# Sixteen-graph network with neighbour dilation: keep-masks written in place with two stores per graph, adjacency rows loaded from ScalarE's queue

## Time and profile before

| | |
|---|---|
| median of 3 runs | 2692.42 us |
| lowest, highest | 2684.85, 2693.45 us |
| the profiled execution, its own time | 2686.08 us |
| its span, first to last instruction | 2684.3 us |
| what lies around the span | 1.8 us |
| mean granted clock of PE | 0.990 of full speed |

### The profile page before, as it was taken

How to read it: one execution, slowest core, us unless ns; L and a number is a source line. 1 busy time by engine, 2 the same in 40 slices (tenths; PEclk the granted TensorE clock), 3 DMA queues, 4 the chain that set the end, 5 groups by cost and what they waited for, 6 DMA issues and landing times. The chain is left out here.

```text
span 2684.3 us, 38830 instructions
## 1 busy us (share of the span) xinstructions
PE 2574.4 (96%) x12390; PEld 1634.7 (61%) x12390; DVE 2082.9 (78%) x5413; ACT 1365.9 (51%) x4060; POOL 598.8 (22%) x265
## 2 busy tenths in 40 slices
PE   6999989999989999999999998999999999999898
PEld 4666656656655666656665664555555555555797
DVE  5788889889889988989989877766666635666676
ACT  4566645665654676646663421332322344443676
POOL 0000000000000000000000003766666603433673
PEclk8999999999999999999999999999999999999999
DMA  7254184364177347157345223555555419996663
GB/s 246 79 164 132 48 201 136 97 158 155 43 197 194 89 146 192 49 157 198 93 113 159 46 69 137 201 192 192 192 191 191 183 55 387 405 404 261 251 234 152
DMA packets 325878, 455.48 MB, mean 170 GB/s; under 512 B 155680, under 2 KB 218528, under 8 KB 325664
## 3 DMA queue, kind: packets, MB, share of 16 engines
q1 hardware_dynamic: 325664, 452.89, 52.4%
HBM read 352.13 MB, written 67.11 MB: 156 GB/s over the span
## 5 line engine op out<-in xcount | busy, mean ns | idle before, releaser
L721 PE MATMUL a_acc<-a_ew,a_Hr 128*128 128x512 f32 x1536 | 754.4, 600 | 0.0
L895 DVE TENSOR_TENSOR a_ew<-adj,a_cos 128x512 f32<-128x512 f32 x768 | 508.0, 681 | 69.0 <-PE a_cos L714 67.1
L712 PE MATMUL a_cos<-a_nh 128*128 128x512 f32 x768 | 417.2, 543 | 31.5 <-DVE a_ew L895 16.4
L721 PEld LDWEIGHTS a_acc<-a_ew,a_Hr 128*128 128x128 f32 x1536 | 275.8, 190 | 153.7 <-issue 110.2
L641 POOL TENSOR_TENSOR a_Au<-a_Ab,tri 128x512 fp8e4<-128x512 fp8e4 x32 | 36.8, 1150 | 1367.2 <-ACT a_Ab L815 1367.2
L832 ACT ACTIVATE a_v<-a_D,a_wb,a_small 128x256 f16<-128x256 f32 x512 | 287.2, 632 | 99.8 <-PE a_D L754 59.9
L714 PE MATMUL a_cos<-a_nh,a_nl 128*128 128x512 f32 x768 | 305.5, 398 | 0.0
L713 PE MATMUL a_cos<-a_nl,a_nh 128*128 128x512 f32 x768 | 302.9, 394 | 0.0
L822 ACT ACTIVATE a_vr<-a_D,a_small 128x128 f16<-128x128 f32 x432 | 161.9, 457 | 134.1 <-DVE a_small L967 133.8
L1387 PE MATMUL b_acc<-adj,b_z 128*128 128x512 f32 x512 | 225.0, 592 | 0.0
L712 PEld LDWEIGHTS a_cos<-a_nh 128*128 128x128 f32 x768 | 146.1, 190 | 127.5 <-DVE a_ew L895 52.7
(11 more groups left out here) (267 smaller groups left out, 4361.3 us busy)
## 6 DMA issues: line engine op xcount, KB each, us to landing
adj<-in_adjT SPq DMA_DIRECT2D x108, 1024.0 KB, 12.6
adj<-in_adjT SPq DMA_DIRECT2D x128, 512.0 KB, 4.0
stage<-in_adj SPq DMA_DIRECT2D x256, 256.0 KB, 3.3
scr_keep<-a_kp SPq DMA_DIRECT2D x256, 64.0 KB, 1.8
scr_z<-b_zT SPq DMA_DIRECT2D x32, 512.0 KB, 3.7
scr_ag<-b_a SPq DMA_DIRECT2D x32, 512.0 KB, 3.3
stage<-scr_keep SPq DMA_DIRECT2D x13, 1024.0 KB, 7.3
b_kp<-scr_keep SPq DMA_DIRECT2D x12, 1024.0 KB, 7.8
```

The costliest lines, as they stand in the source:

```text
L712: e.matmul(cos[j][:], n[:, blk(k)], n[:, half(j)], start=True, stop=False)
L721: e.matmul(acc[j][:], Hr[u % 2][:, k, :], ew[idx % EW][:], start=(k == 0), stop=(k == NK - 1)).then_inc(E["agg"], 1)
L895: e.tensor_tensor(ew[idx % EW][:], adj[g % 2][:, k, half(j)], cos[j][:], ALU.mult).then_inc(E["ew"], 1)
```

## The change

- The mask is written in place: the product goes back to the half row of `TT` that it reads. The three buffers `kp` and the 256 stores go. Once all eight rows of one half of a graph are masked, SP stores that half (512 KB, 4096 bytes of each partition in one piece), two stores per graph, each graph of a quad with a semaphore of its own (`st0` to `st3`). The scratch tensor gets the layout of `TT`, so the second stage reads the masks with a step of two bytes (`masked`), and a graph's masks are 8 KB in one piece on each partition.
- New order constraints: a mask waits for the flips that still read what it overwrites (`flips_ahead`), on the diagonal also for the block's `check`; a flip waits for masks released ahead of it (`masks_ahead`). A `fill` of quads 2 and 3 waits for both stores of its graph in the quad before. A graph's flips and masks at a block are placed graph by graph, all flips ahead of the masks.
- The adjacency rows are loaded by ACT instead of SP: a step `load` in ACT's order, from which the step `row` takes it. The plan has it at 90 ns on ACT and 1000 ns of transfer (before: 70 on SP and 700).
- `PACE` goes from 24 to 22, and there is one more semaphore.

The core of the diff (the fallback `dilate_all`, which this trace doesn't run, gets the same layout):

```diff
-PACE = 24
+PACE = 22
+MASK = 3
-        S["keep"] = nc.dram_tensor("scr_keep", [G, NK, 128, N], U8, kind="Internal").ap()
+        S["keep"] = nc.dram_tensor("scr_keep", [G, 128, NK * N], U8, kind="Internal").ap()
-def readers(quad, i, k):
-    seen = [(q, k // 4) for q in range(NK)] + [(k, 1 - k // 4)]
-    return [("dve", "mask", quad, i, q, j) for q, j in seen]
+def released(m, j):
+    return max(2 * m + 1, 4 * j + 3)
+def crossing(q, j):
+    return [(m, q // 4) for m in (2 * j, 2 * j + 1)]
+def flips_ahead(q, j):
+    return [f for f in crossing(q, j) if released(*f) <= released(q // 2, j)]
+def masks_ahead(m, j):
+    return [(q, h) for q in range(NK) for h in range(2)
+            if (m, j) in crossing(q, h) and released(q // 2, h) < released(m, j)]
...
-            freed = readers(quad - 2, i, k) if quad > 1 else []
+            freed = [("dma", "store", quad - 2, i, j) for j in range(2)] if quad > 1 else []
             for j in range(2):
-                transfer(("row", n, i, j), 700, early + ([("dve", "wide", prev, i, j)] if done else []),
-                         None, "af")
-                add("act", ("row", n, i, j), 540, 2, [("dma", "row", n, i, j)], None, None, "af")
+                add("act", ("load", n, i, j), 90, 2, early + ([("dve", "wide", prev, i, j)] if done else []), None, "af")
+                add("dma", ("load", n, i, j), 1000, 0, [("act", "load", n, i, j)])
+                add("act", ("row", n, i, j), 540, 2, [("dma", "load", n, i, j)], None, None, ("af", ("load", n, i, j)))
...
-                        transfer(("mask", quad, i, q, j), 300, [("dve", "mask", quad, i, q, j)], None, None, "kp")
+            if k == NK - 1:
+                for j in range(2):
+                    transfer(("store", quad, i, j), 1400, [("dve", "mask", quad, i, q, j) for q in range(NK)])
...
+                elif kind == "store":
+                    quad, i, j = a
+                    slot = Q * (quad % 2) + i
+                    wait_masks(e, [("dve", "mask", quad, i, q, j) for q in range(NK)])
+                    if quad and j == 0:
+                        e.wait_ge(T[f"st{i}"], 32 * quad)
+                    e.dma_start(S["keep"][quad * Q + i][:, 4096 * j:4096 * j + 4096],
+                                TT[:, slot, 2 * j:2 * j + 2].rearrange("p m k x s -> p (m k x s)").bitcast(U8)).then_inc(
+                        T[f"st{i}"], 16)
...
+                elif kind == "load":
+                    n, i, j = a
+                    r = nth["act", "load", n, i, j] - 1
+                    if r > 2:
+                        e.wait_ge(T["sign"], nth[("act", "row") + of["act", "load"][r - 3]])
+                    e.dma_start(af[r % 3], A["adj"][n // NK * Q + i, blk(n % NK), half(j)]).then_inc(T[f"af{r % 3}"], 16)
...
-                    e.wait_ge(T[f"fl{r % 4}"], 16 * (r // 4 + 1))
+                    for turn in [r] + [nth[("sp", "flip", quad, i) + f] - 1 for f in flips_ahead(q, j)]:
+                        e.wait_ge(T[f"fl{turn % 4}"], 16 * (turn // 4 + 1))
                     e.wait_ge(T["rw"], nth["dve", "wide", quad * NK + q, i, j])
-                    if c > 2:
-                        e.wait_ge(T[f"kps{c % 3}"], 16 * (c // 3))
+                    if j == q // 4:
+                        e.wait_ge(T["v8"], nth["dve", "check", quad * NK + q])
+                    mine = row_half(slot, j, q)
                     turned = flip[r % 4].bitcast(FP8).rearrange("p (m t) (x s) -> p m t x s", t=2, s=2)
-                    e.tensor_tensor(as_blocks(kp[c % 3][:]), row_half(slot, j, q), turned[:, :, :, :, q % 2], ALU.mult,
-                                    saturate=False).then_inc(T["kp"], 1)
+                    e.tensor_tensor(mine, mine, turned[:, :, :, :, q % 2], ALU.mult, saturate=False).then_inc(T["kp"], 1)
...
+        def masked(b, c, q):
+            row = b[:, q, :].rearrange("p (m s x) -> p m s x", s=2, x=128)
+            return row, row, c.rearrange("p (m k x s) -> p m k s x", m=4, k=NK, s=2)[:, :, q]
```

More of the change, by code:

```diff
@@ L444, in plan_dilation @@
                 add("dve", ("wide", n, i, j), 605, 4, [("act", "wide", n, i, j)], None, None, "v")
-        for m, j in FLIPS:
-            if k == max(2 * m + 1, 4 * j + 3):
-                for i in graphs_of(quad):
+        for i in graphs_of(quad):
+            for m, j in FLIPS:
+                if k == released(m, j):
                     transfer(("flip", quad, i, m, j), 600, [("dve", "wide", quad * NK + b, i, m // 2)
-                             for b in range(4 * j, 4 * j + 4)], "flip", "flip", rank=2)
+                             for b in range(4 * j, 4 * j + 4)] + [("dve", "mask", quad, i) + a for a in masks_ahead(m, j)],
+                             "flip", "flip", rank=2)
+            for m, j in FLIPS:
+                if k == released(m, j):
                     for q in (2 * m, 2 * m + 1):
                         last = ("flip", ("flip", quad, i, m, j)) if q % 2 else None
-                        add("dve", ("mask", quad, i, q, j), 605, 3, [("dma", "flip", quad, i, m, j),
-                            ("dve", "wide", quad * NK + q, i, j)], f"flip{quad}{i}{m}{j}", "kp", last)
-                        transfer(("mask", quad, i, q, j), 300, [("dve", "mask", quad, i, q, j)], None, None, "kp")
+                        add("dve", ("mask", quad, i, q, j), 605, MASK, [("dma", "flip", quad, i, m, j),
+                            ("dve", "wide", quad * NK + q, i, j)] + ([("dve", "check", quad * NK + q)] if j == q // 4 else [])
+                            + [("dma", "flip", quad, i) + f for f in flips_ahead(q, j)], f"flip{quad}{i}{m}{j}", None, last)
+            if k == NK - 1:
+                for j in range(2):
+                    transfer(("store", quad, i, j), 1400, [("dve", "mask", quad, i, q, j) for q in range(NK)])
 def layer0_plan():
@@ L467, in layer0_plan @@
                                        for i in range(Q) for q in range(NK) for j in range(2)] +
-               [("dma", "mask", quad, i, q, j) for q in range(NK) for j in range(2)] + [("act", "row", n, i, j) for n in range(NK * QUADS) for i in range(Q) for j in range(2)])
-    return P.order({"D0": 1, "D1": 1, "af": 3, "v": 3, "kp": 3, "flip": 4}), P.turns["kp"]
+               [("dma", "store", quad, i, j) for j in range(2)] + [("act", "row", n, i, j) for n in range(NK * QUADS) for i in range(Q) for j in range(2)])
+    return P.order({"D0": 1, "D1": 1, "af": 3, "v": 3, "flip": 4})
 def layer0(nc, A, C, S):
@@ L506, in layer0 @@
         v = [P.sb(f"v{i}", [128, 512], F16) for i in range(3)]
-        kp = [P.sb(f"kp{i}", [128, 512], FP8) for i in range(3)]
         small = P.sb("small", [128, 2, 10, Q])
@@ L513, in layer0 @@
         mv4 = C["mv"][:].rearrange("p (g k) -> p g k", k=NK)
-        plan, ring = layer0_plan()
+        plan = layer0_plan()
         nth = {}
@@ L521, in layer0 @@
         of = {(name, kind): [s[1:] for s in steps if s[0] == kind]
-              for name, steps in plan.items() for kind in ("rank", "wide", "mask", "row", "flip")}
+              for name, steps in plan.items() for kind in ("rank", "wide", "mask", "load", "row", "flip")}
         def slots(n):
@@ L550, in users_of @@
             return [("dve", "mask", quad, i, q, j) for q in (2 * m, 2 * m + 1)]
-        every = [("dve", "mask") + a for a in ring]
+        every = [("dve", "mask") + a for a in of["dve", "mask"]]
         def earlier(engine, kind, upto):
@@ L1214, in sp @@
         def sp(e):
-            e.dma_start(C["kp0"].bitcast(U8), S["keep"][ORDER[0]].rearrange("k p n -> p k n")).then_inc(E["load"], 16)
+            e.dma_start(C["kp0"].bitcast(U8), S["keep"][ORDER[0]]).then_inc(E["load"], 16)
             e.wait_ge(E["load"], 16)
```

74 lines of the change are left out of this document (32 added, 42 removed).

## The result

| | before | changed |
|---|---|---|
| median of 4 runs, us | 2690.78 | 2649.84 |
| lowest, highest | 2684.85, 2693.45 | 2646.28, 2653.51 |
| the profiled execution, own time | 2686.08 | 2651.22 |
| its span | 2684.3 | 2649.4 |
| mean granted clock of PE | 0.990 | 0.994 |

With a fourth run the median of the kernel before is 2690.78 us, where three gave 2692.42. The ratio is 0.9851, 95% interval 0.9828 to 0.9874: 40 us, 1.5% faster. The forecast was -18 us (2674, with a range from 2648 to 2704). The direction is right, the size is less than half of what came; the measured time lies 2 us inside the fast end of the range.

The account below looks back on a forecast made before the run. PE, busy 96%, was taken to bound the kernel, with about 46 us of its idle time going with the masks. Terms -25 + 1 + 3 + 0 + 3 + 0 + 0 = -18 us gave 2674 us, range 2648 to 2704.

Parts of the forecast that it names:

- The store waits go: DVE's 42.3 us of waits for mask stores in `layer0` vanish; 60% reaches PE: -25 us, ends -9 and -42.
- The rival in which the waits go in full: DVE's store waits in `layer0` reach PE whole: -42 + 7 = -35, about 2657 us; chance 0.14.
- The mask itself: DVE's mask writes fp8 with a two-byte step, 6 ns more each: +1 us on PE, far end +11.
- The rival in which the masks were the cost: DVE's 164.7 us of mask work stay, only 9 us come back: about 2690 us, no change; chance 0.20.
- The new waits: DVE's masks wait for flips to land: 5 us of DVE, +3 us on PE, bound +24.
- the sign: Sign that the prediction is right: DVE's idle time ended by flips stays under 10 us.
- The loads on ACT: ACT issues 256 adjacency loads instead of SP: +3 us, ends -5 and +20.
- The second stage: It reads masks with a two-byte step; POOL's products take 0.3 us more each, but PE has no idle time: +0.
- Later fills and wider gates: In `layer0` quad 2 starts 25 to 45 us later, `PACE` shifts early gates up to 18 us; both costed at nothing.

Follow-up runs that it names:

- e5: Kernel before, but stores send a constant tile instead of the masks, and SP instead of DVE waits for the earlier store; ratio 0.9909.
- e6: Changed kernel with adjacency rows loaded by SP again (70 and 700 ns in the plan) and `PACE` 24; ratio 0.9892.
- e3: Changed kernel with adjacency rows loaded by SP again (70 and 700 ns in the plan), `PACE` 22; ratio 0.9941.
- g3: Changed kernel with its load's transfer planned at 700 ns in place of 1000; ratio 0.9914.
- f3: Kernel before, loads on SP, with a row's transfer planned at 1000 ns in place of 700; ratio 0.9945.
- f5: Kernel before with loads on ACT, their transfer still planned at 700 ns; ratio 0.9961.
- e4: Kernel before with loads on ACT at the change's plan numbers (90 and 1000 ns), `PACE` 24; ratio 0.9963.
- f4: Changed kernel with each row load split into two of 256 columns, 256 issues more on ACT, same bytes; ratio 0.9927.
- e1: Changed kernel with `PACE` back at 24; ratio 0.9910.
- e2: Kernel before with `PACE` 22 alone; ratio 1.0000.
- e7: Kernel before with loads on ACT (90 and 1000 ns in the plan) and `PACE` 22, masks and stores as before; ratio 0.9952.
- f1: Changed kernel with `PACE` 21.5 in place of 22; ratio 0.9874.
- e8: Kernel before with two mask buffers `kp` instead of three, same stores and order of steps; ratio 1.0353.

## Why the prediction was wrong in size

**The store waits go: -25.** Right. e5 measures -25 us. The rival in which the waits go in full came nearest to the measured time with 2657 us, but its mechanism is out: it asks for -42 us from this term.

**The mask itself: +1.** The mean is 692 ns, 4 more than before, where 6 were taken; the runs can't tell the step of two bytes from none (684 to 700 ns with the buffers, 687 to 703 in place). The rival in which the masks were the cost is out, since e5 and e6 gain 25 and 29 us and still make all 256 masks.

**The new waits: +3.** Mis-sized on DVE: 16.5 us of idle time until a flip landed and 5.9 put to issue, where 5 were taken and under 10 named as the sign. In e6, without the other parts, it is 7.4. These waits grow with the tightness of the rest, and DVE still idles less ahead of masks than before (24.4 us against 47.2). The three terms make -21; e6 measures -29 for them together (24 to 34 by its interval).

**The loads on ACT: +3.** This is the step that failed. It took the load as the same step in another queue, with its issue time as the cost. But in this program a step's number in the plan decides where the steps are placed on every engine, and the move took the number from 700 to 1000. The change's description named it, and the prediction priced it nowhere. Where +3 was taken, the loads with their numbers brought -24 us (e3 against changed), -16 to -17 at the units' end in all four pairs. The number is worth -17 us in the changed kernel (g3 against changed), -15 on the kernel before with loads on SP (f3), and nothing there with loads on ACT (f5 against e4). With the number left at 700 the changed kernel gives 0.9914, -23 us against the forecast of -18, so the rest of the sum is near, if by terms that miss in both directions. The queue alone brings -10 on the kernel before (f5 against before); in place at `PACE = 22` it moves the units' end by +1.4 us (e3 to g3) and takes e3's tail away. Its cost on ACT, bounded at +20, stands only in f4. The Trainium skill says in "DMA: Bandwidth & Descriptors", section "Issuing engines are not separate DMA queues", that the issuing engines share the same 16 DMA engines, so a move saves the issuing sequencer's time alone. The traces agree: landing went from 3.3 to 3.1 us only. That rule is about the queue; the larger part of what the loads brought in the changed kernel came with the number.

**The second stage: 0.** Right. It needs 1057.8 us instead of 1054.2, both inside the 1054 to 1059 of all runs. DVE's masks take 1216 ns; POOL's rise from 2011 to 2130, 0.12 us each where 0.3 were reckoned, hidden.

**Later fills and wider gates: 0.** Right for the changed kernel: quad 2's first `cross` comes 29 us later, where its start was put 25 to 45 later, and the last mask still ends 26 us ahead of the units. But the reason was half of it. The cover is no property of the change, and five kernels next to it (e1, e2, e3, e4, e7), with f1 a sixth, have a tail of 10 to 19 us. `PACE` was set down as worthless; with 24 the changed kernel gives 0.9910, and 22 is worth 16 us in it, as there the order has no tail.

**PE's busy time: in no term.** The sum priced idle time alone. 13 of the 38 us in `layer0` are the same matmuls in less busy time, about half of it by the granted clock, as the windows above show. It is in the measured terms too: from g3 to the changed kernel PE idles 8 us less (41.8 to 33.8) and is busy 10 us less (1521.9 to 1511.9), and seven windows of 10 us below 1.00 become none.

**What stays open.** Why an order made with a longer transfer time is better, with the loads on SP before and in the changed kernel, and no better with the loads on ACT before. It isn't the sum of ACT's waits for rows, which f3 leaves at 98.7 us. What falls step by step with 700, 850, 1000 and 1200 are PE's waits for DVE in `layer0`: 55.0, 43.5, 42.3 and 35.0 us; in the changed kernel they are 44.4, 33.5 and 30.8 us with 700, 1000 and 1050. That signs placed nearer to when their rows come let the work behind them keep its time is argued and not shown; it would need an order in which the signs alone are moved by hand.

## What to carry to other kernels

When a scheduler writes the order, read the changed cost numbers of a diff as edits in their own right, and test them alone first: here the run of one number (f3) shows 15 us. A number for a transfer should be held against its landing time in the trace (700 ns in the plan, 3.3 us on the chip). When parts don't add up in time, compare them at the marks inside the span, here the units' end, and look for a second chain, as the tail was, that takes over at the end; but a mark of one execution is good for a few us at best. And compare the busy time of the bounding engine as well as its idle time: where the count of instructions is the same and the time isn't, look at the granted clock.

## What was unexpected of the hardware

An issue on ACT can run beside ACT's compute. The timeline of ACT in the changed kernel:

```profile
742.41 0.64 ACT L855 ACTIVATE a_v<-a_D,a_wb,a_small 128x256 f16<-128x256 f32 x1 [6.49 <-DVE a_T L1033]
742.46 0.84 ACTq L831 DMA_DIRECT2D stage<-in_adj  x2
742.91 0.62 ACT L855 ACTIVATE a_v<-a_D,a_wb,a_small 128x256 f16<-128x256 f32 x1
```

Two issues of together 0.84 us stand over two running activations, and yet doubling all issues cost 20 us.

Waits of DVE cost clock, too. With two buffers (e8) the mean granted clock is 0.980 instead of 0.990. The window of that kernel from 40 us to the units' end (PE clock is the third number from the end), and from 300 to 400 us; below it the kernel before from 300 to 400 us:

```profile
40.00:1727.00 1687.00, 1562.61 (x7667) 988.35 (x7665) 1374.59 (x3696) 913.63 (x2543) 36.89 (x32) 0.98 0.44 119
```

```profile
300.00:400.00 100.00, 89.51 (x407) 55.49 (x406) 76.74 (x204) 54.11 (x146) 2.20 (x2) 0.95 0.50 120
```

```profile
300.00:400.00 100.00, 93.24 (x439) 59.36 (x438) 86.43 (x235) 56.93 (x152) 2.19 (x2) 0.98 0.58 137
```

The two kernels have one order of steps and differ in the buffers alone. Against the window of the kernel before in the section on the result PE idles 65.6 us more (124.4 against 58.8) and is busy 37.5 us more, with the same matmuls but for three records. Where the clock is below 1.00, part of the stretch ran at 1.2 GHz instead of 2.4: 26 windows of 10 us in this stretch, against six before. So some of the idle time came back as slower work, and that is why 99 us of waits could cost 95 us, though PE's idle time grew by two thirds of them. That the clock makes all of the 37.5 us isn't shown.

The mean clock of a whole run can mislead here. Of the kernel before, 20 to 30 us shows 0.55, of e8 1.00:

```profile
20.00:30.00 10.00, 3.15 (x11) 2.56 (x12) 1.60 (x3) 6.50 (x23) 0.00 (x0) 0.55 1.03 412
```

```profile
20.00:30.00 10.00, 3.17 (x11) 2.57 (x12) 1.60 (x3) 6.49 (x22) 0.00 (x0) 1.00 1.03 412
```

Up to 40 us PE is busy for 18.9 us in both, so this dip costs nothing. Yet the clock missing there, 0.83 over 40 us in the kernel before and 1.00 in the changed one, is more than half of the difference between the means 0.990 and 0.994.
